# Next rows, absolute values and turned weights a step earlier in a four-layer kernel

## The reference

```
f1: q, k, v projections; softmax over a single score (so 1); attn * v
f2: sigmoid(x @ Q(w1).T) * (x @ Q(w2).T) @ Q(w3).T   with weights rounded to -1, 0, 1, hidden 1408
f3: causal attention, 16 heads, 4 key/value heads, rotary embedding, output projection c_w
f4: h = silu(x @ w_gate) * (x @ w_up), hidden 2048
    in each group of 4 hidden values the 2 with the largest |h| are kept, the others set to 0
    out = h_sparse @ w_down
```

## Time and profile before

| | |
|---|---|
| runs, us | 1392.14, 1392.31, 1400.21 (median 1392.31) |
| profiled execution | 1398.82 us, of which 1397.1 is the span from first to last instruction |
| PE busy | 1331.5 us (95%) |
| DVE busy | 974.8 us (70%) |
| POOL busy | 691.9 us (50%) |
| ACT busy | 664.5 us (48%) |
| stage 2 in the span, roughly | 120 to 420 us |
| stage 4 in the span, roughly | 851 to 1397 us |

### The profile page before, as it was taken

One profiled execution on the slowest core, in us unless ns is written; L12 is line 12 of the kernel. 1 busy time (PEld: TensorE's weight loads), 2 busy tenths in 40 slices (PEclk: granted clock), 3 DMA queues, 4 the chain that ended last, 5 costly groups with the idle time before them and its releaser, 6 DMA issues.

```text
span 1397.1 us, 19464 instructions
## 1 busy us (share of the span) xinstructions
PE 1331.5 (95%) x7206; PEld 914.6 (65%) x7206; DVE 974.8 (70%) x1959; ACT 664.5 (48%) x1153; POOL 691.9 (50%) x836
## 2 busy tenths in 40 slices
PE   6989999999999899999999999999999999999997
PEld 5875446556455454555555457788888788778886
DVE  5998575655666867777666532887668766876687
ACT  6664342232313554455555585546454545454442
POOL 2676231421313324233334367787686668666864
PEclk9999999999997999999999999999999999999999
DMA  9100210203213122143011323123323332332300
GB/s 336 72 1 1 76 61 16 87 4 99 76 48 97 55 47 63 23 118 119 23 55 54 122 91 151 61 104 108 109 91 132 125 114 84 132 120 91 119 33 30
DMA packets 46270, 116.86 MB, mean 84 GB/s; under 512 B 3420, under 2 KB 4448, under 8 KB 42336
## 3 DMA queue, kind: packets, MB, share of 16 engines
q1 hardware_dynamic: 45104, 114.31, 24.3%
q10 hardware_dynamic: 1072, 1.31, 0.3%
HBM read 92.28 MB, written 23.07 MB: 83 GB/s over the span
## 4 chain that ended last, share of the span: by engine, by line
PE 71%; DVE 19%; ACT 5%; issue 2%; POOL 1%; DMA 0%; POOLq 0%; DVEq 0%; ACTq 0%
PE PS L1758 70%; DVE cm L661 5%; DVE SM L677 3%; DVE PS L894 2%; PE PS L1767 2%; DVE SM L673 1%; ACT EX L1328 1%; DVE hm L670 1%; DVE SM L678 1%; DVE hm L661 1%; ACT ws_g L1145 1%; DVE qb L667 1%; DVE SM L667 1%; ACT sl L1148 1%; DVE tm L661 1%
## 5 line engine op out<-in xcount | busy, mean ns | idle before, releaser
L1328 ACT ACTIVATE EX<-PS 128x512 f32<-128x512 f32 (+3 forms) x384 | 170.9, 494 | 139.9 <-PE PS L1758 138.2
L1561 POOL TENSOR_TENSOR ws_g<-rw,ws_g 128x512 fp32r<-128x512 f32 x64 | 136.3, 2129 | 123.6 <-ACT ws_g L1145 123.6
L1561 POOL TENSOR_TENSOR SM<-SM 128x1 f32<-128x1 f32 x128 | 82.7, 646 | 219.7 <-DVE SM L667 216.7
L894 DVE CUSTOM_DVE_ANT_0 PS<-PS,MW 128x128 f32<-128x128 f32 (+3 forms) x256 | 122.5, 503 | 61.8 <-PE PS L1758 61.5
L1758 PE MATMUL PS<-KG,QG 96*128 96x512 f32 (+3 forms) x384 | 135.4, 386 | 18.8 <-DVE SM L894 7.7
L1677 POOL TENSOR_SCALAR_AFFINE_SELECT EX<-EX 128x128 f32<-128x128 f32 x256 | 75.2, 304 | 157.3 <-ACT EX L1328 154.9
L1530 ACT ACTIVATE ab<-hm 128x512 f32<-128x512 f32 x64 | 40.5, 633 | 210.8 <-DVE hm L661 210.8
L1758 PE MATMUL PS<-QG,KG 98*128 98x512 f32 (+3 forms) x384 | 132.3, 380 | 3.2 <-ACT EX L1328 2.7
L1758 PE MATMUL PS<-ws_d,HH 128*128 128x512 f32 x528 | 125.7, 389 | 0.7 <-DVE HH L661 0.7
L1758 PEld LDWEIGHTS PS<-QG,KG 98*128 98x128 f32 x384 | 70.5, 193 | 71.8 <-issue 45.1
L661 DVE TENSOR_TENSOR cm<-cm 128x512 bf16<-128x512 bf16 (+1 forms) x136 | 115.1, 877 | 2.4
(11 more groups left out here) (203 smaller groups left out, 2782.1 us busy)
## 6 DMA issues: line engine op xcount, KB each, us to landing
rw<-in_L_ffn_w_gate SPq DMA_DIRECT2D x16, 1024.0 KB, 5.1
rw<-in_L_ffn_w_up SPq DMA_DIRECT2D x16, 1024.0 KB, 5.3
rw<-in_L_ffn_w_down SPq DMA_DIRECT2D x16, 1024.0 KB, 7.1
QG<-qs SPq DMA_DIRECT2D x48, 256.0 KB, 4.2
raw<-in_L_ffn_w SPq DMA_DIRECT2D x3, 2816.0 KB, 11.6
qs<-stg SPq DMA_DIRECT2D x16, 512.0 KB, 3.9
xA<-xs SPq DMA_DIRECT2D x2, 2048.0 KB, 7.7
ys<-xA SPq DMA_DIRECT2D x4, 1024.0 KB, 4.3
```

The lines of the kernel that those rows point to most:

```text
L894: last = e.tensor_tensor_reduce(out=p, in0=p, in1=MW[:, 512 - k1 + k0:512], scale=1.0, scalar=BIG, op0=ALU.add, op1=ALU.max, accum_out=m1)
L1328: e.activation(EX[:, n % 16, 0:W], PS[:, score_bank(n), 0:W], ACT.Exp, scale=ISQ, bias=0.0).then_inc(S["ex"], 1)
L1561: return e.tensor_tensor(out, a, b, op)
```

## The change

Three things move, and nothing is added or taken away.

1. Stage 2: the jobs ("q", 0) to ("v", 0) run in steps 9 to 14 instead of 10 to 15.
2. Stage 4, rows of the next block: SP's load of xb comes in step 9 of a block instead of 10 (between the loads of gate and up), and the statistics on DVE and POOL in step 11 instead of 12. For block 1 the load is earlier anyway and only the statistics move.
3. Stage 4, ACT: the absolute value is taken behind the three weight splits of its step, except in each fourth step (s % 4 == 3), where it stays ahead of them.

```diff
-        jobs = {10 + c: ("q", c) for c in range(4)}
-        jobs.update({14: ("k", 0), 15: ("v", 0), 18: ("c", 0), 20: ("c", 1), 22: ("c", 2), 23: ("c", 3)})
+        jobs = {9 + c: ("q", c) for c in range(4)}
+        jobs.update({13: ("k", 0), 14: ("v", 0), 18: ("c", 0), 20: ("c", 1), 22: ("c", 2), 23: ("c", 3)})
...
-                if s % 16 == 10 and 0 < k < 3:
+                if s % 16 == 9 and 0 < k < 3:
                     w.wait_ge(S["d_out%d" % ((k + 1) % 2)], 16)
                     w.wait_ge(S["d_ys1"], 32)
                     e.dma_start(xb[(k + 1) % 2][:, :, :], ys_h[:, 4 * (k + 1):4 * (k + 1) + 4, :]).then_inc(
...
-                if k < 3 and s % 16 == 12:
+                if k < 3 and s % 16 == 11:
                     for i in range(4):
                         w.wait_ge(S["d_xb%d" % ((k + 1) % 2)], 16 * ((k + 1) // 2 + 1))
                         stats(96 + 4 * (k + 1) + i, xb[(k + 1) % 2][:, i, :], EPS, "mv7")
...
+            def absolute(s):
+                w.wait_ge(S["hm"], s + 1)
+                w.wait_ge(S["cma"], s // 4)
+                e.activation(ab4[:, s % 4, :], hm4[:, s // 4 % 2, s % 4, :], ACT.Abs, scale=1.0, bias=0.0).then_inc(
+                    S["ab"], 1)
...
-                w.wait_ge(S["hm"], s + 1)
-                w.wait_ge(S["cma"], s // 4)
-                e.activation(ab4[:, s % 4, :], hm4[:, s // 4 % 2, s % 4, :], ACT.Abs, scale=1.0, bias=0.0).then_inc(
-                    S["ab"], 1)
+
+                if s % 4 == 3:
+                    absolute(s)
                 if s > 0:
                     split_w("g", s + 3)
                 split_w("u", s + 3)
                 split_w("d", s - 4)
+                if s % 4 != 3:
+                    absolute(s)
...
-                if k < 3 and s % 16 == 12:
+                if k < 3 and s % 16 == 11:
                     for i in range(4):
                         n = 4 * (k + 1) + i
                         stats(96 + n, "mv7", "rs7", n)
```

## The result

Timed beside each other, the changed kernel took 1407.44 us (median of 7 runs, 1404.40 to 1412.68) and the kernel before 1400.21 (7 runs, 1392.14 to 1401.03). The ratio is 1.0072, 95% interval [1.0047, 1.0097]: slower by 0.7%, where 0.4% faster was forecast. (Ratios are given here as they were recorded for the two sets of runs; the quotient of two medians can differ from them by 0.1 or 0.2%, here it is 1.0052.) The profiled execution took 1409.58 us with a span of 1407.8, against 1398.82 and 1397.1, so there are 10.7 us of span to explain.

A forecast was written before the change was run, and what follows sets the result against it. PE was taken to bound stage 4 (busy 465.5 of 473 us), with 9.2 us of waits as ceiling. Terms -1.8 - 0.3 + 0.7 - 3.2 - 0.4 = -5.0 took 1392.3 to 1387.3 us; forecast 1384.5 to 1389.5 (chance 0.40), full range 1382 to 1395.

The forecast's parts named there:

- Stage 2: Turned weights a step sooner: PE's wait for VW goes, -1.8 us, at worst 0.
- Rows and statistics: Stage 4, a step sooner: PE's 0.85 us waits for normed rows at steps 30 and 46 go; hm(28) at least 3 us sooner.
- The feared delay by the xb load: Stage 4: the sooner load delays the "up" weight, ACT's high half waits some 3 us, hm(26) perhaps 1 us.
- Steps 30 and 46: Stage 4, blocks 1 and 2: PE waits 1.0 instead of 2.6 us, gain 1.6 each, together -3.2.
- Absolute values behind the weights: Stage 4, ACT's order: waits of ACT, POOL and PE's 1.5 us at step 8 go; DVE pays beside POOL.
- the price of POOL's new supply: Stage 4, DVE: counts and products lengthened by 1.3 us per POOL instruction met, +2.6 to +6.5 per group, taken as +4.
- B: Rival: DVE blocked behind POOL in stage 4, eight counts taking 13.6 us, +17.1 us, 1409; half the supply some 1396; chance 0.08.
- My sign for A: Next profile, stage 4: counts staying near 6.8 us would mean that the rival A holds instead of the forecast.
- A: Rival: every wait goes, POOL's supply fills only DVE's idle time, -9.2 us, 1383.1; chance 0.15.
- C: Rival: stage 4 wins nothing because counts take what statistics and waits give; only stage 2 gains, 1390.5; chance 0.20.
- D: Rival: the sum is right, but the median execution has the low clock stretch early in stage 3, 1394; chance 0.17.
- The tail: End of stage 4: ACT's last silu is freed of one weight split of about 0.6 us, -0.4, range -0.7 to 0.

The follow-up runs named there:

- e1_turned: Kernel before with only stage 2's turned weights made a step sooner; 1397.93 against 1397.66 us, ratio 0.9994.
- e2_rows: Kernel before with only stage 4's xb load and row statistics a step sooner; 1396.20 against 1397.66 us, ratio 0.9973.
- e5_turned_rows: Changed kernel with absolute values put back ahead of the weights on ACT; 1394.41 against 1394.60 us for the kernel before, ratio 0.9992.
- e3_abs: Kernel before with only the absolute values moved behind the weight splits on ACT; 1425.57 against 1397.66 us, ratio 1.0188.
- e11_gate_alone: Kernel before plus only a wait of POOL until DVE's low halves are done; 1396.69 against 1394.58 us, ratio 1.0000.
- e4_gate: Changed kernel with POOL's weight halves in steps 4g+1 held until counts and products are done; 1419.90 against 1397.66 us for the kernel before, ratio 1.0151.

## Why the prediction was wrong

**Stage 2 (-1.8 us): right in mechanism, not measurable.** The wait is gone in every kernel with the new `jobs`; by the ratio of `e1_turned` the gain is 0.8 us, with an interval from 3.5 won to 1.7 lost.

**Rows and statistics (-0.85 at steps 30 and 46, hm 3 us sooner): the waits go, but there was little to win.** With them in place no kernel that keeps the old order on ACT waits for rows or hm at steps 30 and 46. But `e1_turned`, without them, does not wait for rows either, and for hm 0.25 and 0.22 us there. In time, `e2_rows` shows 3.8 us by its ratio, and `e5_turned_rows`, which has the same, 1.1 with an interval across 0; in stage 4 itself `e2_rows` is 0.3 us shorter than `e1_turned`. A gain beyond that is not settled. The feared delay by the xb load did not show.

**Steps 30 and 46 (-3.2 together): the base was one execution's.** The 2.6 us at each were read from the profiled run, where a comparison was blocked for 8.09 us; the lump of three took 9.83 us at step 28 and again at step 44. `e1_turned` has the same code in stage 4, and there:

```profile
1069.02 6.77 DVE L661 TENSOR_TENSOR cm<-ab 128x1536 bf16<-128x1536 f32 x3 [0.70 <-ACT ab L1530]
...
PE PS L1758 <- DVE hm L661: 0.5, 2, 0.2
```

The comparisons took 6.77 us, not 9.83, PE waited 0.5 us for hm in all, and for the normed rows not at all. Of the 5.0 us of my sum more than 3 had nothing to be taken from: the 3.2 were waits of one execution, and I took them off the median of others.

**Absolute values behind the weights (step 8 -0.3, step 14 +0.7, tail -0.4): the failed step.** The term that failed is the price of POOL's new supply on DVE: charged to the wrong instructions, it came out at nearly nothing where PE pays it. I wrote that this supply costs "+2.6 to +6.5 us on DVE per group; I take +4", and laid it on counts and products only. Per group of four steps the means give counts 8 x 0.105 = 0.8, products 4 x 0.40 = 1.6, casts 4 x 0.26 = 1.0, low halves 4 x 0.59 = 2.4, comparisons 3 x -0.27 = -0.8: +5.0 in all. Against `e5_turned_rows` it is +5.2, with next to nothing for counts and comparisons. So the total was close, which is luck; its place was wrong. Counts, the main bearer in my sum, bear almost nothing of it, and over half (3.4 of 5.0, and 6.1 in step 10) falls on the step that makes HH, for which the prediction has no term. In the trace of before POOL stood there, but because of the very wait that the change removes. At step 14 I counted with DVE idle standing some 4 us ahead of hm(11), room for the statistics; the longer halves of step 10 had taken that room first, and PE waited 4.13 us where I had +0.7, range up to +1.5. At step 8 the two waits, for hm(5) and hm(6), are 2.47 + 1.38 - 1.53 = +2.3 where I had -0.3, beyond the end of my range (+0.4); hm(6) is late by the low halves (5.22 for 2.49). At steps 31 and 47 the changed kernel waits 1.91 and 1.88 us for turned rows, which DVE makes behind the same halves; before it was 0.2 each, and the prediction does not look there. Without the sooner statistics PE waits 5.33, 6.64 and 6.65 us for hm in the next-to-last steps (14, 30, 46) of the first three blocks of `e3_abs`.

**The clock: left out.** The sum has no term for what a wait does to the clock: +3.0 us here behind one of 4.13, and another 1.7 behind the 1.88 of step 47, where the next twelve matmuls took 4.57 us instead of 2.9. In `e3_abs` the waits in stage 4 (OT left out) come to 23.9 us against 8.0 in before, 15.9 more, while the span is 26.4 longer (1423.5 against 1397.1), at a mean clock of 0.981 against 0.993; against `e1_turned`, in stage 4 alone, it is 28.3 longer, 20.6 of them waits. That the rest is the clock is read from these figures, not tried by itself.

**The rivals.** B was right in kind: the kernel got slower, and because DVE is held up beside POOL. It rests on the Trainium skill's "SBUF — State Buffer", "Who interferes with whom", on instructions with two inputs in SBUF, and products and low halves, which have them, were lengthened. B's prices for steps 8 and 14 (+2.9 and about +5) are near what came, +2.3 and +4.1 of waits. But it charged them to eight counts of 1.7 us, and the eight took 7.0 to 8.6 us in the lumps of steps 5, 9, 13 and 29, not 13.6; and most of its time of 1409 (+5.5 each) was worked out for steps 30 and 46, which lost nothing, upon a base 7.9 us below the one measured. That 1409 is near 1407.44 is luck. I gave B 0.08 because I asked only for how many POOL instructions arrive between comparisons and hm of the next step. That was the wrong place to count. My sign for A, counts that stay near 6.8 us, nearly came (6.99 at step 29), and A was false: the sign watched the instructions that did not matter. A and C fell. D supposed low clock ahead of stage 4 in the longer runs of before. The runs of before bear that out in part: on the chip of `e5_turned_rows` those at a mean clock of 0.996 or 0.997 took 1391.0 to 1394.6 us, those at 0.992 or less 1395.0 to 1403.5. For the profiled execution it was wrong: its 6 us stood in stage 4, and its low clock early in stage 3 (0.82 from 447 to 464 us, rows 11) is found in `e2_rows` too, at 0.68. D does not explain the loss.

**The base.** 1392.31 was the median of three runs. Seven had 1400.21, and 23 to 29 on other chips 1394.58 to 1397.66. Of the 20.1 us between 1387.3 and 1407.44, 7.9 are the base and 12.2 the sum: -5.0 where +7.2 was measured. The tail (-0.4) went the other way too: 0.84 for hm in block 3 and 0.9 for HH where there was 0.7 for HH alone. Two small slips change nothing: 33.18 / 6 is 5.5 and not 5.6, and 0.5 to 1.8 us of delay less 1.5 give -1.0 to +0.3 at step 8, where the range is put at -1.5 to +0.4.

## What to carry over

When a wait goes that held back a second engine, look at the times when that engine stood idle: these are where the first engine ran undisturbed, and the next instructions there must be priced as contended too, not only those that were contended before. A stall that shows in one profiled execution need not be in the next: here the 9.83 us of comparisons stood in two blocks of one execution, but neither in `e1_turned` nor in `e11_gate_alone` (6.77 and 6.93 at step 28), so look for it in a second execution before counting on it. If a reorder helps one engine and slows another, a wait on the offender's side (here POOL until the low halves are done) can undo the harm; here it was as good as giving up the reorder (0.9979 and 0.9992 against 0.9992), and no better beyond the noise.

## What the runs showed of the hardware

- Casts have one input, in SBUF, and yet POOL slowed them as it did instructions with two: 6.25 us for four in `e4_gate`, 1.42 alone. They take 0.42 us each for 512 columns where a subtraction takes 0.68, which would fit a faster mode; the trace does not name the mode. The Trainium skill, "SBUF — State Buffer", "Who interferes with whom", says that casts can run in a mode that uses both ports and then contend with GpSimd; the 6.25 us agree, and the prediction used only its sentence on two inputs.
- Against a full POOL queue DVE and POOL mostly took turns: one DVE instruction for each POOL instruction of 1.5 to 1.8 us. Not always: the comparison of 8.09 us in the kernel before stood until five POOL instructions in a row were through. In one place it was POOL that lost: at 922.39 us in the kernel before, its first instruction behind a pause took 3.38 us, while the low halves beside it ran at their normal 1.29 us for two. Behind pauses of 3.42 and 3.34 us in the changed kernel (898.04 and 923.92 us) it took 1.68 and 1.84 us, so the pause is not the reason.
- Behind a wait of PE of 4.13 us a stretch of 10 us had a granted clock of 0.70. Behind those of 2.47 and 1.38 the matmuls took 2.98 and 2.97 us, so nothing was lost but the wait; of two waits of 1.9 us one was followed by 0.88 (1240 to 1250 us) and one by 1.00 (1100 to 1120 us). The length of a wait alone does not tell what it costs.
